# Expert stage of a mixture-of-experts block: slots of 256 rows, gate and up as one fp32 product per block of weights, programs written out

## The reference

```python
probs = jax.nn.softmax(xf @ router_w.T, axis=-1)       # 8192 rows, 8 experts
topv, topi = jax.lax.top_k(probs, 2)                   # two experts a row
...
g = jnp.einsum('nd,edf->nef', xf, gate_w) + gate_b     # 128 -> 256
u = jnp.einsum('nd,edf->nef', xf, up_w) + up_b         # 128 -> 256
h = jax.nn.silu(g) * u
expert_out = jnp.einsum('nef,efd->ned', h, down_w) + down_b   # 256 -> 128
y = jnp.einsum('ne,ned->nd', probs, expert_out)
```

## Time and profile before

| | us |
|---|---|
| median of 3 runs | 1877.77 |
| lowest, highest | 1873.24, 1881.41 |
| the profiled execution, its own time | 1875.53 |
| its span, first to last instruction | 1873.8 |

### The profile page before, as it was taken

How to read it: one execution, slowest core, us unless ns; L and a number is a source line. 1 busy time by engine, 2 the same in 40 slices (tenths; PEclk the granted TensorE clock), 3 DMA queues, 4 the chain that set the end, 5 groups by cost and what they waited for, 6 DMA issues and landing times. The chain is left out here.

```text
span 1873.8 us, 42058 instructions
## 1 busy us (share of the span) xinstructions
PE 1460.5 (78%) x11453; PEld 1120.5 (60%) x11454; DVE 1275.8 (68%) x3937; ACT 813.4 (43%) x2049; POOL 941.4 (50%) x1140
## 2 busy tenths in 40 slices
PE   3799999999999999972199999466666636999980
PEld 2567777777777777752077777344444424777760
DVE  4469999898999888752455555357777763555547
ACT  1135555454555545440044444256666633444430
POOL 2124545665666666557145555315655563555540
PEclk9559999999999999885599999777777767999995
DMA  6101111111111111001322222201112112222229
GB/s 167 47 33 44 44 38 45 50 50 48 51 50 50 50 50 50 30 15 41 111 65 71 71 70 71 58 26 56 59 55 60 50 36 63 70 71 73 71 60 269
DMA packets 143847, 116.64 MB, mean 62 GB/s; under 512 B 20736, under 2 KB 132432, under 8 KB 143696
## 3 DMA queue, kind: packets, MB, share of 16 engines
q1 hardware_dynamic: 114672, 74.25, 13.9%
q0 software_dynamic: 16896, 35.16, 5.6%
q10 hardware_dynamic: 12128, 5.39, 1.1%
HBM read 46.48 MB, written 40.97 MB: 47 GB/s over the span
## 5 line engine op out<-in xcount | busy, mean ns | idle before, releaser
L1004 DVE TENSOR_REDUCE mx<-max_banks 128x6 f32<-128x768 f32 x256 | 243.4, 951 | 51.8 <-PE max_banks L755 50.9
L1312 ACT ACTIVATE p<-ebuf 128x768 f32<-128x768 f32 x256 | 216.1, 846 | 92.4 <-DVE ebuf L1033 92.2
L1033 DVE TENSOR_TENSOR ebuf<-score_banks,bias 128x768 f32<-128x768 f32 x256 | 243.5, 951 | 15.7 <-PE score_banks L781 11.0
L1724 POOL DMA_INDIRECT choice_rows<-first_yo,first_xg x136 | 130.2, 958 | 157.8 <-DVE first_yo L1854 150.8
L1724 POOL DMA_INDIRECT choice_rows<-second_yo,second_xg x136 | 130.2, 957 | 140.0 <-DVE second_yo L1854 137.0
L2169 POOL DMA_INDIRECT expert_rows<-z_d_rows,z_d_index x128 | 128.0, 1000 | 63.7 <-issue 29.7
L1573 POOL DMA_INDIRECT expert_rows<-a_d_rows,a_d_index x128 | 129.4, 1011 | 31.7 <-issue 27.1
L743 PE MATMUL max_banks<-identb,biasb 128*128 128x128 bf16 x512 | 108.3, 234 | 21.0 <-DVE mx L1004 13.9
L800 PE MATMUL bankO<-p,vaug 128*32 128x256 f32 (+1 forms) x2048 | 116.2, 347 | 2.2 <-ACT p L1312 2.1
L1848 DVE TENSOR_TENSOR second_hid<-second_bgu,second_silu 128x256 f32<-128x256 f32 x136 | 57.8, 425 | 86.1 <-ACT second_silu L1810 51.8
L1502 POOL TENSOR_TENSOR rs<-arg,neghalf 128x2 f32<-128x2 f32 x32 | 22.3, 697 | 185.0 <-DVE arg L1071 185.0
(11 more groups left out here) (346 smaller groups left out, 4463.4 us busy)
## 6 DMA issues: line engine op xcount, KB each, us to landing
first_xg<-expert_rows SPq DMA_DIRECT2D x136, 66.0 KB
second_xg<-expert_rows SPq DMA_DIRECT2D x136, 66.0 KB
qs<-hi SPq DMA_DIRECT2D x64, 128.0 KB
ks<-hi SPq DMA_DIRECT2D x64, 128.0 KB
z_rows<-choice_rows SPq DMA_DIRECT2D x64, 128.0 KB
c_rows<-choice_rows SPq DMA_DIRECT2D x32, 256.0 KB
qs<-lo SPq DMA_DIRECT2D x32, 128.0 KB
ks<-lo SPq DMA_DIRECT2D x32, 128.0 KB
```

The costliest lines, as they stand in the source:

```text
L1004: nc.vector.reduce_max(mx[:, n, places:places + 5:4, :], max_banks[:, :, 0:BK].rearrange("p h (k c) -> p h k c", k=3), AXX).then_inc(maxed ...
L1033: nc.vector.tensor_tensor(ebuf[:, half_of_ebuf(c, j), :, :], score_banks[:, :, 0:BK], bias32[:, plain(j), :], ALU.add).then_inc(scores_fre ...
L1312: nc.scalar.activation(p32[:, j % 4, :, :], ebuf[:, half_of_ebuf(c, j), :, :], ACT.Exp).then_inc(exped, 1)
L1724: pool.indirect_dma_start(choice_dram, bass.IndirectOffsetOnAxis(ap=xg[:, i % G, E:E + 1].bitcast(I32), axis=0), yo[:, i % 4, :], None,).t ...
```

## The change

A slot now holds 256 rows (`Q`), and there are 72 slots in place of 136 tiles. Inside an expert stage:

- ACT copies the gate and up weights of the slot's expert, 512 columns, to one of two fixed places `wgu`, and x transposed to `xT`. PE multiplies blocks of 128 weight columns by 256 rows in plain float32, four products a slot, with features as outputs and rows along the columns. Nothing is split, and there is no bias product.
- Silu takes the gate bias as a column; DVE adds the up bias column and multiplies in one instruction. The result is already turned as the down product needs it, so the transposes of `hid` and the copy of them are gone.
- The down product has four float32 products a slot, `yo` is 256 rows, and POOL stores it with two indirect transfers.
- PE, ACT and DVE programs are written out over all 72 slots; the expert register is loaded every 4 slots, on ACT too.

Outside:

- `pad` is gone. Setup writes 2048 padding rows to device memory twice, `pad_rows` and the end of `expert_rows`, each from POOL's zeroed `d.rows`, the second after the first has landed. The setup block waits for both.
- `pad_rows` copies 256 rows a list from device memory to device memory.
- `expert_weights` has no splits; PE turns the biases into columns. The tables have 72 entries.

```diff
-        self.CAP = self.N + P
+        self.Q = 2 * P
+        self.CAP = self.N + self.Q
-        self.SLOT_TILES = -(-(2 * self.TILES + self.NE - 1) // self.BODY) * self.BODY
+        self.SLOTS = -(-(2 * self.N // self.Q + self.NE - 1) // self.BODY) * self.BODY
...
+                for j, rows_dram in enumerate((pads_dram, slots_dram[s.NE * s.CAP:s.NE * (s.CAP + s.Q), :])):
+                    sp.wait_ge(pads_made, j + 1)
+                    sp.dma_start(rows_dram.rearrange("(n p) c -> p n c", p=P), d.rows[:].rearrange("p b t c -> p (b t) c")).then_inc(pads_left, 16)
                 sp.wait_ge(x_in, 64)
                 sp.wait_ge(rel_tab, 16)
+                sp.wait_ge(pads_left, 32)
...
-                nc.gpsimd.memset(w["pad"][:], 0.0).then_inc(filled, 1)
+                labels = d.rows[:, :, :, s.E:s.E + 1].rearrange("p b t a -> p (b t a)").bitcast(I32)
+                nc.gpsimd.tensor_copy(labels, pad_f[:, 0:2 * s.NE]).then_inc(pads_made, 1)
+                pool.wait_ge(pads_left, 16)
+                nc.gpsimd.tensor_copy(labels, pad_f[:, 2 * s.NE:4 * s.NE]).then_inc(pads_made, 1)
...
-                for e in range(NE):
-                    ch.step(nc.vector.tensor_copy(w["hi"][:, e, :], raw[:, e, :]))
-                    last = ch.mark(nc.vector.tensor_tensor(w["lo"][:, e, :], raw[:, e, :], w["hi"][:, e, :].bitcast(F32),
-                                                           ALU.subtract))
...
-        first = engine.value_load(w["pad_at"][0:1, e:e + 1], min_val=0, max_val=s.NE * s.CAP - P)
-        engine.dma_start(slots_dram[bass.ds(first, P), :], w["pad"][:, e, :]).then_inc(padded, 16)
+        first = engine.value_load(w["pad_at"][0:1, e:e + 1], min_val=0, max_val=s.NE * s.CAP - s.Q)
+        engine.dma_start(slots_dram[bass.ds(first, s.Q), :], pads_dram[e * s.Q:(e + 1) * s.Q, :]).then_inc(padded, 16)
...
+                def gate_up(i):
+                    pe.wait_ge(w_ready, i + 1)
+                    pe.wait_ge(xT_done, i + 1)
                     for f in range(NF):
+                        if i >= 2:
+                            pe.wait_ge(hid_done, i * NF + (f + 1 - 2 * NF))
+                        for k in range(2):
+                            at = slice(k * EF + f * P, k * EF + (f + 1) * P)
+                            dst = bgu[i % 2 * NF + f][:, k * 2 * P:(k + 1) * 2 * P]
+                            last = nc.tensor.matmul(dst, wgu[:, i % 2, at], xT[:, i % 2, :], start=True, stop=True)
+                        last.then_inc(gu_full, 1)
...
+                for i in range(ST):
+                    if i % 4 == 0:
+                        e = experts_around(pe, i)
+                    transpose_x(i)
+                    if i >= 3:
+                        down(i - 3, e(i - 3))
+                    if i >= 1:
+                        gate_up(i - 1)
...
+                def take_weights(i, e):
+                    if i >= 2:
+                        act.wait_ge(gu_full, i * NF - 2)
+                    nc.scalar.copy(wgu[:, i % 2, :], w["gate_up"][:, bass.ds(e, 1), :].rearrange("p a f -> p (a f)")).then_inc(w_ready, 1)
```

More of the change, by code:

```diff
@@ new lines, in down @@
+                def down(i, e):
+                    pe.wait_ge(hid_done, i * NF + NF)
+                    if i >= 2:
+                        pe.wait_ge(y_done, i - 1)
+                    for t in range(2):
+                        for f in range(NF):
+                            last = nc.tensor.matmul(by[i % 2][:, t * E:(t + 1) * E], hT[:, i % 4, f, t * P:(t + 1) * P],
+                                                    w["down"][:, bass.ds(e, 1), f, :].rearrange("p a d -> p (a d)"),
+                                                    start=(f == 0), stop=(f == NF - 1))
+                    last.then_inc(y_full, 1)
@@ new lines, in silu @@
+                def silu(i):
+                    act.wait_ge(b_ready, i + 1)
+                    for f in range(NF):
+                        act.wait_ge(gu_full, i * NF + f + 1)
+                        if i >= 1:
+                            act.wait_ge(hid_done, i * NF + (f + 1 - NF))
+                        nc.scalar.activation(act_[:, f, :], bgu[i % 2 * NF + f][:, 0:2 * P], ACT.Silu,
+                                             bias=biases[:, i % 4, f:f + 1]).then_inc(silu_done, 1)
+                for i in range(ST):
+                    if i % 4 == 0:
+                        e = experts_around(act, i)
+                    take_weights(i, e(i))
+                    take_x(i)
+                    if i >= 1:
+                        silu(i - 1)
@@ new lines, in hidden @@
+                def hidden(i):
+                    if i >= 4:
+                        dve.wait_ge(y_full, i - 3)
+                    for f in range(NF):
+                        dve.wait_ge(silu_done, i * NF + f + 1)
+                        nc.vector.scalar_tensor_tensor(hT[:, i % 4, f, :], bgu[i % 2 * NF + f][:, 2 * P:4 * P],
+                                                       biases[:, i % 4, NF + f:NF + f + 1], act_[:, f, :], ALU.add, ALU.mult
+                                                       ).then_inc(hid_done, 1)
```

303 lines of the change are left out of this document (104 added, 199 removed).

## The result

The kernel after takes 1858.8 us (median of 20 runs, 1842.3 to 1881.1), beside 1875.6 us for the kernel before in the same session (20 runs). The ratio is 0.992, 95% interval [0.990, 0.995]. Times here are medians of all runs, and ratios compare runs of one session, those in the chip's faster state alone. The kernel is faster, by 0.8% instead of the 5% that was forecast, and 1858.8 lies far above the range that ended at 1808. The profiled execution has a span of 1840.6 us (time 1842.3), against 1775.9 in the sum. It is the fastest of the 20, so the trace explains its own 65 us and not the 16 us by which the median lies above it.

A forecast was written before the change was run, and what follows sets the result against it. TensorE, busy 39.1 of 40 us, was taken to set the pace in the expert stages. 1873.8 - 96.5 (expert stages) - 4.1 (expert weights) + 2.7 (setup) = 1775.9 us of span, forecast 1778 us, range 1763 to 1808.

The forecast's parts named there:

- the sum: Whole kernel's span: 1873.8 less 96.5 (expert stages) and 4.1 (expert weights), plus 2.7 (setup), giving 1775.9 us.
- the covers: Expert stages: other engines' work hides beside 2.87 us a slot; ACT 1.9, DVE 1.5, POOL 2.5 us.
- rivals B and C: GpSimd's stores bound the expert stages: B 2035 us, chance 0.03; C, mildly, 1797 us, chance 0.07.
- Work of a slot: TensorE in the expert stages: 2.83 us of work and 0.04 us of gaps a slot, 2.87 in all.
- Rival A: Expert stages: gaps per register load stay as long, 0.34 us more a slot; 1826 us, chance 0.12.
- Rival D: Expert stages: weights copy lands late and PE waits each slot, 3.47 us a slot; 1864 us, chance 0.04.
- Start and end of a stage: Expert stage from SP's first load to POOL's last store: 216.8 us, against 265.5 before.
- Expert weights: Block before the first expert stage: shorter tables, bias transfers gone, padding issue 8.04 us as now; 4.1 us gained.
- Setup: Setup block ends later because the second padding transfer lands at 44.6: 2.7 us lost, from 0 to 6.
- Second stage's padding: End of the recurrence: the same edits lie beside POOL's scatter, so they gain nothing.
- rival C: Expert stages: POOL a mild bound at 3.0 us a slot; 1797 us, chance 0.07.

The follow-up runs named there:

- stores 1.27 against 1.57 us apart: Kernel after with a GpSimd memset behind every store, 16 columns (1.27 us apart) against 400 (1.57 us): 1868.4 us against 1838.5 us.
- more stores in the kernel before: Kernel before with one more indirect store for every fourth tile, to a spare place: 1973.3 us, ratio 1.048 to before.
- the paced kernels: Kernels with a GpSimd memset behind every store to space the stores; kernel after with 112 columns took 1776.4 us, with 208 columns 1783.2 us.
- stores at 1.41 us: Kernel after with a GpSimd memset of 208 columns behind each store, in a later session: 1783.2 us, ratio 0.953 to before.
- stores at 1.33 and 1.41 us: Kernel after with a GpSimd memset of 112 or 208 columns behind each store, in later sessions: 1776.4 us and 1783.2 us.
- plain stores: Kernel after with GpSimd's two stores a slot as plain transfers to fixed rows, sorting back left out: 1770.2 us, ratio 0.948 to before.
- one indirect store a slot: Kernel after with one indirect store to a spare place and one plain store a slot, sorting back left out: 1810.3 us, ratio 0.963.
- in order: Kernel after with the indirect stores' row numbers fixed and in order, sorting back left out: 1859.9 us, ratio 0.994 to before.

## Why the prediction was wrong

**The step that failed** is the one on the covers: "POOL: ... 2 x 1.26 = 2.5 us: beside 2.87 this hides, with little to spare", and with it that ScalarE and VectorE have "over 2 us in hand". GpSimd's time was right to 0.01 us, and it was not the bound. I asked only whether GpSimd would be the bound (rivals B and C priced it as one) and not what its work does to others. The term missing is the held updates: (3.35 - 2.82) x 71 = 38 us in the first stage and (3.26 - 2.82) x 71 = 31 in the second, 69 us together, against the 64.7 by which the span of 1840.6 exceeds the sum. From SP's first load to the last store the stages took 254.0 and 248.7 us instead of 216.8 each.

**How it feeds itself.** Stores that follow at 1.26 us hold TensorE's updates. Silu, product and the taking of y then come late and in a bunch; GpSimd gets two or three slots' results at once and stores them back to back, 4 to 8 in a run; which holds the next updates. The bursts of updates come 0.6 to 1.35 us after the end of the store ahead of them, 1.0 in the median of the first stage. The loop is seen in the timeline; that closeness starts it is shown by stores 1.27 against 1.57 us apart, and by more stores in the kernel before.

**The rest, by the steps of the sum:**

- Work of a slot, 2.83 us and 0.04 of gaps: 2.84 in the gapless steps, 2.82 on average where no update is late. The gaps are less than assumed. Rival A (gaps at register loads) is wrong: TensorE's loads are still there in the paced kernels.
- ScalarE's and VectorE's prices: weights copy 0.62 for 0.58, x copy 0.38 for under 0.4, silu 0.47 and product 0.48 as assumed, `yo` 0.42. Rival D (late weights copy) is wrong: no wait for `wgu` in 200 us.
- Start and end of a stage, 216.8 us with its slots: with stores at 1.41 us SP's first load is at 930.1 and the last store ends at 1146.1: 216.0.
- Expert weights, gain 4.1 us: from the first load of weights to SP's first load of rows it was 903.42 to 928.21 and is 904.17 to 926.09, 2.9 us gained. The eight transfers within device memory issue in 11.29 us, not 8.04, a price that I had taken over unasked; the shorter tables gained 4.2 us instead of 2.7, which gave half of it back. To set beside the earlier trace rows:

```profile
910.50 0.17 DVE L292 CAST expert<-first_t_ex_w 1x18 int32<-1x18 f32 x1
911.72 11.29 SPq L1671 DMA_DIRECT2D expert_rows<-pad_rows  x8
926.09 3.87 SPq L1848 DMA_DIRECT2D first_xg<-expert_rows  x4
```

- Setup, loss 2.7 us: attention's first instruction moved from 42.41 to 44.68, 2.3 us.
- Second stage's padding, nothing: from the end of GpSimd's scatter to SP's first load it was 5.5 us and is 5.5.

With stores at 1.33 and 1.41 us, where no update was late, the spans are 1777.5 and 1781.9 us against the sum of 1775.9. The mechanism that was forecast is right and its size too; what was wrong is that nothing else would come of it.

The range failed because its upper end was made from doubts about the prices of work. (That end doesn't follow from its own terms either: 1778 + 14 + 7 is 1799, and rival C's 19 us in place of the 14 make 1804. It changes nothing here.) The kernel was moved from stores every 1.89 us to two in 2.84. In the expert stages before, at most three stood under 1.3 us apart. But the attention stage of before already had updates up to 1.7 us late behind close stores, and VectorE waiting 1.34 us for one with its product done. That stage, read as closely as the expert stages, would have given this a rival of its own.

## What to carry to other kernels

When a change makes an engine's work denser, ask two things: whether the engine becomes the bound, and whether anything in the trace has run at that density beside the work that binds. Where an engine waits although its input was finished, compare the moment at which the semaphore rises with the end of the instruction that raises it before looking at the instructions themselves. Where indirect stores from GpSimd stand back to back beside a busy TensorE, try to pace them: a memset of 400 columns behind each gave 1838.5 us where one of 16 gave 1868.4, in one session. Shorter ones looked better still, 1776 us with 112 columns, but in sessions that had no late updates anywhere. Run the unpaced kernel beside the paced one in each session, and use a stage that you didn't touch as a control: without both, a cure and a quiet session look the same.

## What the hardware showed

- TensorE's semaphore updates came 0.01 us behind the modelled end of the matmul where nothing held them, and up to 4.6 us behind it (985.80 for 981.22 in the table above) while GpSimd made indirect stores 1.26 or 1.27 us apart. In executions whose attention stage had late updates, none of 576 recorded in the expert stages was over 1 us late with plain stores, none of 444 with one indirect store a slot, and one of 363 with stores 1.57 us apart (each kernel makes 576, and the trace keeps the rest from us). In attention they came up to 1.7 us late in before behind two stores 1.39 us apart. ScalarE's and VectorE's updates were not held. The Trainium skill ("Perfetto Trace Analysis", on the Tensor Engine instruction) puts the update behind PSUM's acknowledgement that all bytes are written; the trace has no record of it, so no run here tells whether the acknowledgement or the update behind it was held.
- SyncE was slow at times too: in the first stage of after 21 of its register and load instructions took over 0.5 us, most about 0.7, where nearly all take up to 0.3. Seven of them ended within 0.15 us of the start of a burst, the others farther off. Before has 9, eight of them ending 1.25 us behind a store's end; plain stores and one indirect store a slot have none.
- Whether an execution has late updates at all varied by session: thirteen traces have 5 to 23 in attention, the four of two later sessions none, with the same stores there. What decides it is open, and so is the distance between 1.27 and 1.57 us at which they end in the expert stages.
- I see no queue of the DMA engines that grows: in the run of after that holds 981.03, each store's bytes start to move 1.53 to 1.59 us behind its start, for the last as for the first. The fourth store of the next run took 2.1 us, so it isn't excluded for all. That the making of the transfers on GpSimd does it is shown by exclusion (in order or scattered the same, plain not), not by a record of what is blocked.
- An indirect store of 128 rows takes GpSimd 0.96 us, a plain one of the same bytes 0.54.
